# Attention's first norm and first projections computed inside the expert stage; the second batch's norm spread over attention's steps

## The reference, cut to what matters

```python
x = x + 0.5 * _L1_ffn_ref(_layernorm(x, axis=-1), ...)   # 16 experts, top 4, and a shared one
x = x + _L1_attn_ref(_layernorm(x, axis=-1), ...)        # 16 heads of 64
x = x + 0.5 * _L1_ffn_ref(_layernorm(x, axis=-1), ...)
```

```python
m = jax.nn.softmax(dots, axis=-1)
diag = jnp.diagonal(m, axis1=-2, axis2=-1)
keep = jnp.abs((diag - mu) / sd) <= Z_THRESH
masked = jnp.where(valid, dots, NEG)
attn = jax.nn.softmax(masked, axis=-1)
```

## Time and profile before

| | before |
|---|---|
| median of 3 runs | 1868.86 us (1862.9 to 1870.64) |
| the profiled execution | 1873.35 us, span 1872.1 us |
| PE busy | 1778.6 us, 95% |
| DVE, ACT, POOL busy | 70%, 62%, 63% |
| granted PE clock, mean | 0.981 |
| expert stage t = 0 | about 588 to 688 us |
| attention, from the first mean to the first score | 688.6 to 712.6 us |

### The profile page before, as it was taken

How to read it: one execution, slowest core, us unless ns; L and a number is a source line. 1 busy time by engine, 2 the same in 40 slices (tenths; PEclk the granted TensorE clock), 3 DMA queues, 4 the chain that set the end, 5 groups by cost and what they waited for, 6 DMA issues and landing times. The chain is left out here.

```text
span 1872.1 us, 29675 instructions
## 1 busy us (share of the span) xinstructions
PE 1778.6 (95%) x10975; PEld 1215.5 (65%) x10975; DVE 1315.9 (70%) x2491; ACT 1154.4 (62%) x1719; POOL 1175.5 (63%) x665
## 2 busy tenths in 40 slices
PE   8998999988998987999999999999999999999899
PEld 5884444344776754677777777777777777765466
DVE  5626889996555655676777777777777777788676
ACT  5326778853454557676776667666767676753554
POOL 5551778974643540477676777767767777677355
PEclk9999999999999999999999999999999999999999
DMA  3000000001000003212121212121212121200100
GB/s 101 1 1 1 1 0 1 1 0 51 0 1 1 1 26 78 61 48 60 48 61 47 62 48 61 48 61 48 61 48 61 48 61 48 58 24 13 51 6 18
DMA packets 43664, 66.02 MB, mean 35 GB/s; under 512 B 24768, under 2 KB 26176, under 8 KB 43264
## 3 DMA queue, kind: packets, MB, share of 16 engines
q1 hardware_dynamic: 43056, 63.54, 13.2%
q10 hardware_dynamic: 432, 0.59, 0.1%
q0 software_dynamic: 32, 0.00, 0.0%
HBM read 29.05 MB, written 1.24 MB: 16 GB/s over the span
## 5 line engine op out<-in xcount | busy, mean ns | idle before, releaser
L2661 POOL TENSOR_TENSOR at_e_lo<-at_e,at_e_hi 128x1024 fp32r<-128x1024 f32 x256 | 612.8, 2394 | 305.9 <-DVE at_e_hi L2636 297.0
L2418 ACT ACTIVATE at_e<-at_ps,at_dropped 128x1024 f32<-128x1024 f32 x256 | 285.7, 1116 | 222.4 <-PE at_ps L2129 205.6
L2515 DVE CUSTOM_DVE_ANT_0 at_ps<-at_ps,at_mask 128x1024 f32<-128x1024 f32 x256 | 313.4, 1224 | 5.9 <-PE at_ps L2249 3.0
L2408 ACT ACTIVATE at_ps<-at_ps,at_neg_diag 128x1024 f32<-128x1024 f32 x256 | 278.6, 1088 | 39.0 <-DVE at_neg_diag L2506 38.2
L2636 DVE CAST at_e_hi<-at_e 128x1024 fp32r<-128x1024 f32 x256 | 232.7, 909 | 23.2 <-ACT at_e L2418 19.9
L2208 PE MATMUL at_ps<-at_kq,at_qk 64*128 64x512 f32 x768 | 224.0, 399 | 9.5 <-DMA at_kq<-at_qk 3.5
L2258 PE MATMUL at_ps<-at_qk,at_kq 64*128 64x512 f32 x768 | 224.8, 399 | 1.6 <-DVE at_row_max L2515 1.2
L2129 PE MATMUL at_pv_ps<-at_e_hi,at_v_hi 64*128 64x512 f32 x980 | 225.5, 453 | 0.4 <-issue 0.2
L2259 PE MATMUL at_ps<-at_kq,at_qk 64*128 64x512 f32 x768 | 224.8, 399 | 0.0
L2209 PE MATMUL at_ps<-at_qk,at_kq 64*128 64x512 f32 x768 | 224.3, 399 | 0.0
L441 POOL TENSOR_TENSOR ffn_lo<-ffn_hid,ffn_hi 128x512 fp32r<-128x512 f32 x96 | 127.5, 1330 | 127.5 <-DVE ffn_hi L352 127.5
(11 more groups left out here) (437 smaller groups left out, 4172.1 us busy)
## 6 DMA issues: line engine op xcount, KB each, us to landing
at_kq<-at_qk SPq DMA_DIRECT2D x128, 256.0 KB, 4.0
at_mask<-at_mask_dram SPq DMA_DIRECT2D x32, 256.0 KB, 3.6
at_recips<-at_recip_row SPq DMA_DIRECT2D x31, 256.0 KB, 4.4
ffn_h_raw<-in_h SPq DMA_DIRECT2D x2, 1024.0 KB, 7.6
at_head_w_raw<-in_w_qkv SPq DMA_DIRECT2D x32, 64.0 KB, 3.9
x<-in_x SPq DMA_DIRECT2D x4, 256.0 KB, 4.8
moe_gate_in<-in_gate_in SPq DMA_DIRECT2D x2, 512.0 KB, 3.4
moe_up_in<-in_up_in SPq DMA_DIRECT2D x2, 512.0 KB, 4.3
```

What stands on the lines that cost most here:

```text
L2408: act.eng.activation(ps[:], ps[:], ACT.Exp, scale=SCALE, bias=m.small["neg_diag"][s][:, blk:blk + 1], accum_out=m.small["sums"][s][:, blk: ...
L2418: act.eng.activation(m.e[e % 2][:], slot("turned_scores", h, blk)[:], ACT.Exp, scale=SCALE, bias=m.small["dropped"][h % SLOTS][:, blk:blk ...
L2515: dve.eng.tensor_tensor_reduce(out=ps[:], in0=ps[:], in1=m.mask[h % 2][:], scale=1.0, scalar=-BIG, op0=ALU.add, op1=ALU.max, accum_out=m.s ...
L2661: pool.eng.tensor_tensor(m.e_lo[e % 3][:], m.e[e % 2][:], m.e_hi[e % 3][:].bitcast(F32), ALU.subtract).then_inc(sem["at_lo"])
```

## The change

The first batch's norm for attention, the queries and keys of heads 0 and 1 and the split of the value weights move into the expert stage t = 0. They are issued at fixed g by `attention_ahead_*`, which the four engines' expert loops call. The second batch's norm is spread over attention's steps t = 1 to 37. Its two chunks share wide tiles (`pair_*`): the variance is copied out of PSUM, Ln and Exp run once over 1024 columns, and Square runs per chunk. The expert stage's own norm of chunks 2 and 3 uses the same helpers, with ACT's table load after `silu(3)` and not after `silu(1)`, and with logits at g = 7, scores at g = 8, rounding at g = 9 and 10. PE no longer waits for x at the end of the stage, and the loop over t starts at 0. SP issues the head and value weights once the feed-forward stage has ended; the output weights follow after the moves for head 1. The fillers of 7 and 27 matmuls are gone. Tiles get other places in memory.

```diff
+def pair_variance_out(act, c, n, ps, var):
+    act.wait_ge(c.sem["norm_var"], n + 1)
+    act.eng.activation(var, ps, ACT.Copy).then_inc(c.sem["norm_logs"])
+def pair_inverse(act, c, first, var, inv):
+    act.wait_ge(logs, 3 * first + 2)
+    act.eng.activation(inv, var, ACT.Ln, bias=c.eps[:, 0:1]).then_inc(logs)
+    act.wait_ge(logs, 3 * first + 3)
+    act.eng.activation(inv, inv, ACT.Exp, scale=-0.5).then_inc(logs)
+def pair_square(act, c, first, inv, sq):
+    act.wait_ge(c.sem["norm_logs"], 3 * first + 4)
+    for half in HALF:
+        act.eng.activation(sq[:, half], inv[:, half], ACT.Square).then_inc(c.sem["norm_logs"])
+def pair_finish(dve, c, first, j, var, dst, inv, sq):
+    dve.wait_ge(c.sem["norm_logs"], 3 * first + 5 + j)
+    dve.eng.scalar_tensor_tensor(sq, var, c.eps[:, 0:1], sq, ALU.add, ALU.mult).then_inc(done)
...
 def turn(ch):                                      # moe_pe
+        if a and ch >= 2:
+            pe.wait_ge(sem["norm_logs"], 3 * AHEAD_N + ch - 1)
         moe_turn(pe, c, m, t, ch, m.banks[ch % 2])
...
         if p == 0 and ch == 0 and t == 0:
-            pe.wait_ge(sem["norm_done"], 3 * (n0 + 2) + 1)
+            pe.wait_ge(sem["norm_logs"], 3 * (n0 + 2) + 1)
...
-    pe.wait_ge(sem["x_moe"], (t + 1) * NCH)
+    if not a:
+        pe.wait_ge(sem["x_moe"], (t + 1) * NCH)
-MOE_LATER_LOGITS, MOE_LATER_ROUND, MOE_LATER_REST = 5, (4, 5), (5, 6)
-MOE_SCORES_AT = (6, 2)
+MOE_LATER_SQUARE, MOE_LATER_FINISH, MOE_LATER_LOGITS = 4, (4, 5), 7
+MOE_LATER_ROUND, MOE_LATER_REST = (9, 10), (10, 11)
+MOE_SCORES_AT = (8, 2)
...
         norm_square(act, c, n0 + 3, m.xn[3], m.inv[3])     # moe_act, t == 0
+        pair_variance_out(act, c, n0 + 2, m.banks[0], m.pair[0][:, HALF[0]])
         round_hidden(0)
         silu(1)
+        pair_variance_out(act, c, n0 + 3, m.banks[1], m.pair[0][:, HALF[1]])
+        silu(2)
         round_hidden(1)
+        silu(3)
+        round_hidden(2)
         load_logs(act)
-        for ch in range(2, NCH):
-            norm_inverse(act, c, n0 + ch, m.banks[ch % 2], m.inv[ch], m.sq[ch])
+        pair_inverse(act, c, n0 + 2, m.pair[0], m.pair[1])
...
+AHEAD_MEANS, AHEAD_CENTRES, AHEAD_SQUARES = {12: 0, 20: 1}, {12: 0, 20: 1}, {13: 0, 21: 1}
+AHEAD_VARIANCES, AHEAD_VARIANCES_OUT = {14: 0, 22: 1}, {15: 0, 23: 1}
+AHEAD_INVERSE, AHEAD_SQUARED = 23, 24
+AHEAD_FINISHES, AHEAD_ROUNDS, AHEAD_RESTS = {25: 0, 27: 1}, {26: 0, 28: 1}, {27: 0, 29: 1}
+AHEAD_HEAD_W = {14: 0, 16: 1}
+AHEAD_QK = {31: (0, 0), 32: (1, 0), 33: (0, 1), 34: (1, 1)}
+AHEAD_VALUES_HI, AHEAD_VALUES_LO = 17, (18, 19)
+LATER_MEANS, LATER_CENTRES, LATER_SQUARES, LATER_VARIANCES, LATER_VARIANCES_OUT = 1, 2, 3, 7, 8
+LATER_INVERSE, LATER_SQUARED = 27, 28
+LATER_FINISH, LATER_ROUND, LATER_REST = (30, 32), (33, 35), (36, 37)
...
+def attention_ahead_pe(c, a, m, g):                # after expert_out(g - 2)
+    if g in AHEAD_QK:
+        h, half = AHEAD_QK[g]
+        pe.wait_ge(sem["x_moe"], 3)
+        pe.wait_ge(sem["at_w_lo"], h + 1)
+        pe.wait_ge(sem["at_xn_lo"], half + 1)
+        if done := list(AHEAD_QK).index(g):
+            pe.wait_ge(sem["at_qk_lo"], done)
+        products(pe, m.banks[0], True, True, (hi, lo), (a.xn_hi[:, COLS[half]], a.xn_lo[:, COLS[half]])).then_inc(sem["at_qk"])
+def attention_ahead_act(c, a, m, g):               # after silu(g), round_hidden(g - 1)
+    if g in AHEAD_VARIANCES_OUT:
+        pair_variance_out(act, c, AHEAD_N + ch, m.banks[ch], a.pair[0][0][:, HALF[ch]])
+    if g == AHEAD_INVERSE:
+        load_logs(act)
+        pair_inverse(act, c, AHEAD_N, a.pair[0][0], a.pair[0][1])
+    if g == AHEAD_SQUARED:
+        pair_square(act, c, AHEAD_N, a.pair[0][1], a.pair[0][2])
+def attention_ahead_sp(c, a):
+    sp.wait_ge(sem["x_ffn"], 2 * NCH)
+def attention_later_norm_pe(c, m, t):
+    if t == LATER_MEANS:
+        for ch in range(2, NCH):
+            pe.wait_ge(sem["x_moe"], NCH)
+            norm_mean(pe, c, m.pv_ps[:, HALF[ch % 2]], c.x[:, COLS[ch]])
+    if t == LATER_VARIANCES:
+        for ch in range(2, NCH):
+            norm_variance(pe, c, AHEAD_N + ch, m.pv_ps[:, HALF[ch % 2]], m.pair[1][1][:, HALF[ch % 2]])
...
-                    if h == 1:
-                        fill_wait(pe, c, m.ps[2][:, HALF[0]], 27)
```

More of the change, by code:

```diff
@@ L1607, in moe_act @@
     for g in range(MOE_G):
-        if g >= 2:
+        if a:
+            attention_ahead_qk_hi(c, a, m, g)
+        if g >= (2 if t else 4):
             silu(g)
-        if g >= (3 if t == 0 else 1):
+        if g >= (1 if t else 4):
             round_hidden(g - 1)
+        if t == 0 and g == MOE_LATER_SQUARE:
+            pair_square(act, c, n0 + 2, m.pair[1], m.pair[2])
+        if a:
+            attention_ahead_act(c, a, m, g)
         if t == 0 and g in MOE_LATER_ROUND:
@@ L1654, in moe_dve @@
             weighed_product(g)
-        for ch in range(2, NCH):
-            finish(ch)
     else:
@@ L1674, in moe_dve @@
         ch, p = divmod(g, PAIRS + 1)
+        if a:
+            attention_ahead_qk_lo(c, a, m, g)
         if g >= 2:
             weighed_product(g)
+        if t == 0 and g in MOE_LATER_FINISH:
+            j = MOE_LATER_FINISH.index(g)
+            pair_finish(dve, c, n0 + 2, j, m.pair[0], m.xn[2 + j], m.pair[1], m.pair[2])
+        if a:
+            attention_ahead_dve(c, a, m, g)
         if p == MOE_ADDED_AT and ch:
@@ L1829, in qk_due @@
     at = due(t, AT_QK)
-    return at[0] if at and at[0] not in EARLY_QK else None
+    return at[0] if at and at[0] >= 2 and at[0] not in EARLY_QK else None
 def group_due(t):
@@ L2089, in spread_recip @@
         sp.eng.dma_start(m.recips[:], m.recip_row.broadcast_to([HD, SEQ])).then_inc(sem["recip_spread"], 16)
+    for h in range(2):
+        move_parts(h)
+        load_weights(h + 2)
+    sp.wait_ge(sem["x_moe"], NCH)
+    sp.eng.dma_start(m.w_out[:], c.dram["w_out"]).then_inc(sem["attn_load"], 16)
     for t in range(AT_FIRST, AT_LAST):
@@ L2675, in attention_pool, with attention_tiles, sb, places @@
     pool.wait_ge(sem["x_attn"], ATTN_SUMS)
-def attention(nc, c):
+AHEAD_SCRATCH_PLACE = 130368
+def attention_tiles(nc, mem):
+    def sb(name, shape, dt=F32, where=mem):
+        return where.enter_context(nc.sbuf_tensor(name, shape, dt))
+    m = Core()
+    m.qk, m.kq = [None] * SLOTS, [None] * SLOTS
+    def places(*slots):
+        for i in slots:
+            m.qk[i] = sb(f"at_qk_{i}", [P, 2, SEQ], F32R)
+            m.kq[i] = sb(f"at_kq_{i}", [P, 2, SEQ], F32R)
+    m.head_w_raw = [sb(f"at_head_w_raw{i}", [P, 2, HD]) for i in range(2)]
+    m.head_w = [(sb(f"at_head_w_hi{i}", [P, 2, HD], F32R), sb(f"at_head_w_lo{i}", [P, 2, HD], F32R)) for i in range(2)]
+    hi_at = nc.sbuf_base
+    m.xn_hi = sb("at_xn_hi", [P, TOK], F32R)
+    second_var = nc.alloc_sbuf_tensor_at("at_variances_second", [P, SEQ], F32, offset=hi_at + 4 * SEQ)
+    lo_at = nc.sbuf_base
+    m.xn_lo = sb("at_xn_lo", [P, TOK], F32R)
+    first_var = nc.alloc_sbuf_tensor_at("at_variances", [P, SEQ], F32, offset=lo_at)
+    second_xn = nc.alloc_sbuf_tensor_at("at_xn_second", [P, SEQ], F32, offset=lo_at + 4 * SEQ)
+    places(0)
+    m.wv_hi = sb("at_wv_hi", [P, HEADS * HD], F32R)
+    m.wv_lo = sb("at_wv_lo", [P, HEADS * HD], F32R)
+    m.w_out = sb("at_w_out", [P, HEADS // 2, P])
+    places(*range(2, SLOTS))
+    m.minus = sb("at_minus", [P, P], F32R)
+    m.shift = [sb(f"at_shift_row{i}", [P, CH], F32R) for i in range(2)]
+    scratch_at = max(nc.sbuf_base, AHEAD_SCRATCH_PLACE)
+    m.v_hi = sb("at_v_hi", [P, BLK, GROUP, 2, HD], F32R)
+    assert scratch_at + 4 * 2 * SEQ <= nc.sbuf_base
+    first_scratch = nc.alloc_sbuf_tensor_at("at_first_scratch", [P, 2, SEQ], F32, offset=scratch_at)
+    places(1)
+    with ExitStack() as early:
+        m.wv_raw = sb("at_wv_raw", [P, HEADS * HD], where=early)
+        m.xn = sb("at_xn", [P, SEQ], where=early)
+    m.pair = [(first_var[:], first_scratch[:, 0, :], first_scratch[:, 1, :])]
+    m.second_var = second_var
+    m.xn_of = [(m.xn, second_xn)[ch // 2][:, HALF[ch % 2]] for ch in range(NCH)]
+    return m
+def attention(nc, c, m):
     with ExitStack() as mem:
@@ L2729, in attention @@
         m.tiny = sb("at_tiny", [P, 1])
+        second_inv = sb("at_second_inverses", [P, SEQ])
+        m.pair.append((m.second_var[:], second_inv[:], m.heads_out[:]))
         m.last_inv, m.last_step = m.pv_sb, m.e[0]
@@ L2827, in build @@
             ffn(nc, c, 1, first_moe)
-            moe(nc, c, first_moe, 0)
-        attention(nc, c)
+        with ExitStack() as at_mem:
+            at = attention_tiles(nc, at_mem)
+            attention_ahead_sp(c, at)
+            moe(nc, c, first_moe, 0, at)
+            attention(nc, c, at)
         place = Place(nc, (nc.sbuf_base + 31) // 32 * 32, 1)
```

256 lines of the change are left out of this document (138 added, 118 removed).

## The result

The changed kernel takes 1862.2 us (median of six runs, 1855.03 to 1863.07); the kernel before took 1867.97 us on the same chip (1862.9 to 1870.64). The ratio is 0.9966, 95% interval 0.995 to 0.9982: 0.34% faster, inside the 0.5% that the forecast called no difference. The forecast was 1860.9 us, range 1853 to 1873. The profiled execution took 1862.15 us, its span is 1860.9 (before: 1873.35 and 1872.1).

The account below looks back on a forecast made before the run. PE was taken to set the expert stage's pace, every added matmul paid. The opening's -25.0 us and the other terms summed to -8.0, from 1873.35 to 1865.4 us profiled, 1860.9 as median; range 1853 to 1873.

Parts of the forecast that it names:

- Opening: Between last expert product and attention's first score: all 25.0 us removed, the move ready 1.3 us before PE asks.
- PE's added work: Expert stage: two means, two variances and four half projections find no PE gap, +6.2 us (low bound 3).
- Own norm: Expert stage's norm of its own, moved behind silu(3): 1.5 us gained of 5.8; a 3.1 us pause stays.
- Detour: ACT's table loads, Ln and Exp at g = 23 pause PE 3.3 us; DVE's finishes add 1.8; +5.1 us.
- Clock: Expert stage, slow PE behind the pause from g = 23: half of an earlier 1.5 us loss, +0.7 us.
- Finishes and port: Expert stage: four DVE finishes can each wait for a 1.3 us POOL lo part, +1.5 us (0 to 5).
- Attention's start: Means on PE at t = 1, centres on DVE, variances at t = 7 delay ACT's chain, +1.5 us.
- Steps 27 to 37: Attention: DVE's work at t = 30 and 32 exceeds idle time and meets POOL, +2.5 us (0 to 5.5).
- Own time against median: Whole kernel: the median lies 4.5 us below the profiled execution, so 1865.4 us profiled gives 1860.9.
- all hidden: Rival, chance 0.24: idle engines hide the work, no port met, no clock lost, own norm gains 2.5; 1856.7 us.
- Port in turns: Rival, chance 0.12: DVE and POOL take turns at every finish in expert stage, own norm and attention; 1868.4 us.
- Pauses take the clock down: Rival, chance 0.12: pauses at g = 5, g = 25, t = 30 each lose 4.9 us clock; 1874.9 us.

Follow-up runs that it names:

- the doubling: Changed kernel with the four sets of three query and key matmuls at groups 31 to 34 issued twice; stage 115.48 us against 112.66.
- without tables: Changed kernel with two copies replacing the logarithm, exponential and both table loads at g = 23; median 1860.04 us, ratio 0.9955.
- the changed kernel's second: Second profile of the changed kernel, run again with no edit; median 1861.29 us, ratio 0.9963 to the kernel before.
- thirteen matmuls: Changed kernel with thirteen matmuls of unread result in the TensorE pause at g = 5; stage 115.33 us, 2.7 worse.
- own norm back: Changed kernel with only the expert stage's own later norm in its old order; stage 114.20 us, median 1863.44 us, ratio 0.9968.

## Why the prediction was right

Term by term (before: three profiles; changed: those in which the place is unaltered).

- **Opening, -25.0.** Last addition to first score was 24.8 to 25.1 us and is now -0.98: 25.7 to 26.0. Shown. The margin was smaller than forecast: from the last projection matmul of head 0 (690.27 us) to the landing of its last transfer went 7.7 us, not 7.1. The last expert product came 8.4 us behind that matmul, as forecast, but the first score already 7.9. In place of 1.3 us the margin was 0.13 to 0.17 us in ten profiles (0.9 with queries and keys twice). A stage that ends sooner behind g = 33 would, by these numbers, gain hardly more than that.
- **The stage, +13.0 in the sum** (6.2 + 1.0 + 5.1 + 0.7 - 1.5 + 1.5): 112.0 or 112.7 against 99.3 to 99.6, so 12.5 to 13.4. The sum holds, its parts less. *PE's added work* at full price: shown by the doubling. *Turn of chunk 2*: 0.77 to 1.06 us. *Own norm*: at the first addition to x the new order is 2.1 to 2.7 us ahead; undoing it costs 1.5 to 2.2 at the stage's end. *Detour*: the pause of 3.3 came as 3.07, but the 5.1 charged to it are not its own; without tables nothing is won. *Clock, +0.7*: the loss was under-sized. It is 5.1 us in the shown profile and 3.4 in the changed kernel's second, against 1.5 (two profiles) and 3.0 (one) before: mostly 1.9 more. But loss and cost are not the same: where more clock was lost, the pauses were shorter, and the time hardly moved. To price it as a term of its own was the weak step of the sum. *Finishes and port*: maxima of 1.66 us as foreseen, yet the pauses grew by only 3.0 to 5.1 us in all. The over-sized pauses and the under-sized clock cancelled; that the sum came out at 13.0 is partly luck. How much the port alone costs was not tried.
- **Attention's start, +1.5**: 2.7 to 3.3, the mis-sized term behind which the runs stand best. The mean matmuls took 1.98 us (L137 at 700.39), near the 1.7 priced, but the step of letting ACT's chain take up part of them failed. The ninth `sums` starts 13.4 us after the first score (10.5 before), and 11.0 us with the means out of the way. Taking them out of the start gives 1.6 to 1.9 back at the first mask, the variances with them 2.2 to 2.4 in all.
- **Steps 27 to 37, +2.5**: third to fourth mask 31.8 to 33.8 against 29.4 to 29.5, so 2.3 to 4.4. From first to seventh mask the changed kernel took 170.5 and 171.3 us (171.1 to 171.4 in the four kernels with edits in the stage alone), against 167.7, 167.9 and 170.1: by the means +2.3, by the medians +3.3.
- **Own time against median, -4.5**: right in kind. The shown profile of before was 1.3 us above the mean of three in this stretch, and had the longer of the two tails.

By the means of three and of two profiles the sum is 13.0 - 25.9 + 3.0 + 2.3 = -7.6 us, and with +3.3 for the last term -6.6, beside 5.8 and 6.9 measured between the medians.

The rivals: *all hidden* fails on the pauses. *Port in turns* had the mechanism right and the price wrong: the engines took turns at all eleven meetings of such operations in the stage, 3.8 and 2.0 us longer in all, but it needed 1868.4 us; how much of the waiting reached TensorE was not tried. *Pauses take the clock down* had the mechanism right and the size wrong: a pause of 3 us was mostly followed by 1.7 us lost, once by none (thirteen matmuls, g = 25) and once by about 3 (own norm back, same place), not by 4.9, and the 4.9 of the earlier trace rows was partly chance. *Late move* did not occur, by 0.14 us. SBUF — State Buffer in the Trainium skill (section SBUF: two separate sides) gives the shared port pair to whichever starts first, for the whole of its operation, be it GpSimd or a VectorE operation with two inputs in SBUF. The trace agrees: each lengthened operation here ends a fixed time after the other engine's, 0.54 to 0.55 us for VectorE and 1.13 to 1.16 us for GpSimd, and both are lengthened because they wait in turn.

## What to carry to other kernels

Where one engine is full, an added matmul costs its whole spacing even when that engine has pauses in the same stage; the pauses come from a chain that it feeds. Ask of a pause who is next in line: taking away its cause, or filling it with idle work, moved both the wait and the low clock by one step and won nothing. Clock that was lost while another engine had a backlog cost little or no time here; don't add it to a sum as if it did. When executions scatter by 11 us and the change is worth 7, compare stretches between marks in several profiles of both kernels.
